# GpSimd takes the bias and residual sums of batch 0 into the scan slots of a decoder layer

## The chip, the cores and the metric

One core of a Trainium2 chip runs one decoder layer in one launch. The metric is the device time of an execution in microseconds. The engines are named as in the profile: PE (TensorE), DVE (VectorE), ACT (ScalarE), POOL (GpSimd), SP (the queue that issues most DMAs).

## The reference, cut to what matters

```python
x = x + attn(layernorm(x))                 # q, k, v, causal softmax, then out @ Wo + bo
x = x + mamba(ctx, z=layernorm(x))         # conv, dt/B/C, selective scan, then y * silu(z)
x = x + ffn(layernorm(x))                  # 16 experts, top 2, and a shared expert
```

x is (4, 512, 512), ctx (4, 512, 256). The scan has 16 states for each of 512 channels. What the change touches is the first line alone: `x + (out @ Wo) + bo` for batch 0, 512 rows of 512 float32 numbers, kept as four tiles of 128 rows.

## The kernel before

Everything is float32 in 128-partition tiles. The stages follow one another: `project` (projections of all batches), `mix` (attention and scan side by side), `close` (output projection of the last batch, gate, norms, shared expert), and then the routed experts.

`mix` is the stage of the change. It runs 128 slots, g = 0 to 127, with three more to drain it. Each engine has its own program with the slots as its loop, and semaphores tie them; nothing reorders the work. A slot holds a piece of attention (one pair of heads, one tile of 128 queries; g % 4 is the tile, and by the causal mask it costs more the higher it is) and two scans of 128 channels by 512 steps.

In slot g, POOL makes product 2g+2 (`weigh`, L763: step size times input times B), adds a state's output into the accumulator (`add`, L771, sum g-3) and makes product 2g+3. The products go into four buffers, so product n waits for scan n-4. DVE takes the maximum of the scores (`top`, L1033), runs scans 2g and 2g+1 (`scan`, L1041; each needs its product from POOL and its decay from ACT) and adds its half of the outputs (`weigh_c`, L1049). ACT makes the decays (L938), the exponentials (L946), copies of transposed tiles (L955), and the weighted copy that POOL's sum reads (L970, two buffers, so copy n waits for sum n-2). PE makes scores (L800, L803), transposes (L818, L857) and the attention sums (L829).

The output projection of batches 0 and 1 rides in the slots, too: L868 from slot 38 on, and ACT copies its half tiles into x1 (L975). Batch 0's are complete at slot 66. Batch 2's is made by PE behind the slots (`project_tail`, L879), batch 3's in `close` (L1514).

The residual has two sums. `with_bias` (L748) is x + bo on POOL, in the place where x lies; `residual` (L1021) adds this to x1 on DVE. For batch 0 `with_bias` runs on POOL in slots 125 to 128 (`EARLY_BIAS`, L740), and `residual` on DVE in slots 128 and 129, with the last two `weigh_c` behind or between them. Then `close` begins on DVE: statistics of batch 0 (L1758, L1764), a square root on ACT (L1671), the normalized rows (L1771), Silu on ACT (L1680), PE's transposes (L1523) and the gate (L1777). On POOL `close` begins with two constants, a wait for the four residuals (L1469), and the bias sums of the other batches, some of them behind waits for ACT and DVE.

SP's queue issues one row of B for all partitions per scan step i (L727), each behind POOL's product 4(i-2)+3. At some steps it issues more: x of batch 0 at step 36, of batch 1 at step 52, the bias bo at step 54 (L717), x of batch 3 at step 56.

Of the kernel before, what the change touches and what calls it, by code (L numbers as in the profile page):

```python
# [631 lines left out]
def mix(nc, d, keep, ctx, first):  # L632
# [3 lines left out]
    def signal(name):  # L636
        return Signal(nc, ctx, "b_" + name)
# [23 lines left out]
    act_da, act_p, act_turn, act_cy = [signal("act_" + n) for n in ("da", "p", "turn", "cy")]  # L661
    dve_max, dve_scan, dve_acc, dve_rinv, dve_out, dve_res = [signal("dve_" + n) for n in ("max", "scan", "acc", "rinv", "out", "res")]
    act_out = signal("act_out")
    pool_dbu, pool_acc, pool_du, pool_xb = [signal("pool_" + n) for n in ("dbu", "acc", "du", "xb")]
    pe_out = signal("pe_out")
    x1 = keep["x1"]
    s_b_all, s_k = keep["s_b_all"], keep["s_k"]
# [21 lines left out]
    def x_rows(b):  # L689
        return (keep["attn"][:, b, :] if b < B - 1 else keep["x1"][b].rearrange("p t c -> p (t c)")).rearrange("p (t c) -> p t c", c=D)  # L690
# [18 lines left out]
    def sync(sp):  # L709
        def load_wo():  # L710
            sp.wait_ge(pool_dbu.sem, pool_dbu.upto(N * KD - 1))
            for k in range(KD):
                sp.dma_start(keep["wo"][:, k, :], d["wo"][k * P:(k + 1) * P, :]).then_inc(keep["s_wo"].sem, keep["s_wo"].tick(k))

        def load_bo():
            sp.wait_ge(pool_dbu.sem, pool_dbu.upto(3 * N * KD - 1))
            sp.dma_start(keep["bo"], d["bo"].rearrange("(a n) -> a n", a=1).broadcast_to([P, D])).then_inc(keep["s_bo"].sem, keep["s_bo"].tick(0))  # L717

        def load_x(b):
            if b < B - 1:  # L720
                sp.wait_ge(pe_out.sem, pe_out.upto(last_out(b, NT - 1)))
            for t in range(NT):
                sp.dma_start(x_rows(b)[:, t, :], d["x"][b, t * P:(t + 1) * P, :]).then_inc(keep["s_x"][b].sem, keep["s_x"][b].tick(1 + t))

        for i in range(2, STEPS):
            sp.wait_ge(pool_dbu.sem, pool_dbu.upto(4 * (i - 2) + 3))
            sp.dma_start(b_all[i % 2][:, :], d["b_flat"][i:i + 1, :].broadcast_to([P, T])).then_inc(s_b_all[i % 2].sem, s_b_all[i % 2].tick(i // 2))  # L727
            if i == N + 1:
                load_wo()
            elif i == 2 * N + 4:  # L730
                load_x(0)
            elif i == 3 * N + 4:
                load_x(1)
            elif i == 3 * N + 6:
                load_bo()
            elif i == 3 * N + 8:
                load_x(B - 1)
        load_x(2)

    EARLY_BIAS = UNITS - 3  # L740

    def bias_at(b, t):
        return NT * (0, 2, 3, 1)[b] + t
# [6 lines left out]
    def gpsimd(pool):  # L750
        def last_batch(j):
            dt, du = [keep[n][B - 1][:, j * T:(j + 1) * T] for n in ("dt", "du")]
            pool.tensor_tensor(du, dt, du, ALU.mult).then_inc(pool_du.sem, pool_du.tick(j))

        def weigh(unit):
            i, k = unit // KD, unit % KD
            if unit == (B - 1) * N * KD:
                pool.wait_ge(pool_du.sem, pool_du.upto(KD - 1))
            if k == 0:
                pool.wait_ge(s_b_all[i % 2].sem, s_b_all[i % 2].upto(i // 2))  # L760
            if unit >= 4:
                pool.wait_ge(dve_scan.sem, dve_scan.upto(unit - 4))
            pool.tensor_tensor(dbu[:, k, :], keep["du"][i // N][:, k * T:(k + 1) * T], b_all[i % 2][:, :], ALU.mult).then_inc(pool_dbu.sem, pool_dbu.tick(unit))  # L763

        def add(n):
            i, t = n // 2, 2 * (n % 2) + 1
            pool.wait_ge(act_cy.sem, act_cy.upto(n))
            if n >= 2:
                pool.wait_ge(pool_acc.sem, pool_acc.upto(n - 2))
            acc = keep["acc"][:, i // N, t * D:(t + 1) * D]  # L770
            pool.tensor_tensor(acc, acc, cy[n % 2][:, :], ALU.add).then_inc(pool_acc.sem, pool_acc.tick(n))  # L771

        pool.wait_ge(first["dve_dt"].sem, first["dve_dt"].upto(4 * B - 1))
        pool.wait_ge(first["pe_rows"].sem, first["pe_rows"].upto(B - 1))
        weigh(0)
        weigh(1)
        for g in range(UNITS + 3):
            if g + 1 < UNITS:
                weigh(2 * g + 2)
            if 0 <= g - 3 < UNITS:  # L780
                add(g - 3)
            if g + 1 < UNITS:
                weigh(2 * g + 3)
            if g < KD:
                last_batch(g)
            if g == EARLY_BIAS:
                pool.wait_ge(keep["s_bo"].sem, keep["s_bo"].upto(0))
            if EARLY_BIAS <= g < EARLY_BIAS + NT:
                with_bias(pool, 0, g - EARLY_BIAS)

    def tensor(pe):
        def scores(unit):
# [221 lines left out]
    def copy_tail(act, t):  # L1014
        act.wait_ge(pe_out.sem, pe_out.upto(HALVES + t))
        act.activation(x1[TAIL][:, t, :], bank[t], ACT.Copy).then_inc(act_out.sem, act_out.tick(HALVES + t))

    def residual(dve, b, t):
        dve.wait_ge(act_out.sem, act_out.upto(last_out(b, t)))
        dve.wait_ge(pool_xb.sem, pool_xb.upto(bias_at(b, t)))  # L1020
        dve.tensor_tensor(x1[b][:, t, :], x1[b][:, t, :], x_rows(b)[:, t, :], ALU.add).then_inc(dve_res.sem, dve_res.tick(NT * b + t))  # L1021

    def normalize(dve, quad):
        b, m = quad // NT, quad % NT
# [4 lines left out]
    def vector(dve):  # L1029
        def top(unit):  # L1030
            n = (unit % NT + 1) * P
            dve.wait_ge(pe_s.sem, pe_s.upto(unit))
            dve.tensor_reduce(neg_max[unit % 2][:, :], sc[:, :, 0:n], AX.X, ALU.max, negate=True).then_inc(dve_max.sem, dve_max.tick(unit))  # L1033

        def scan(unit):
            i, k = unit // KD, unit % KD
            dve.wait_ge(act_da.sem, act_da.upto(unit))
            dve.wait_ge(pool_dbu.sem, pool_dbu.upto(unit))
            if k == 0 and i >= 2:
                dve.wait_ge(pe_y.sem, pe_y.upto(4 * (i - 2) + 3))  # L1040
            dve.tensor_tensor_scan(state[i % 2][:, k, :], da[unit % 2][:, :], dbu[:, k, :], 0.0, ALU.mult, ALU.add).then_inc(dve_scan.sem, dve_scan.tick(unit))  # L1041

        def weigh_c(n):
            i, t = n // 2, 2 * (n % 2)
            dve.wait_ge(pe_y.sem, pe_y.upto(2 * n))
            if n >= 2:
                dve.wait_ge(dve_acc.sem, dve_acc.upto(n - 2))
            acc = keep["acc"][:, i // N, t * D:(t + 1) * D]
            dve.scalar_tensor_tensor(acc, yb[0][:, :], keep["c_flat"][:, i * NT + t:i * NT + t + 1], acc, ALU.mult, ALU.add).then_inc(dve_acc.sem, dve_acc.tick(n))  # L1049

        dve.wait_ge(first["pe_q"].sem, first["pe_q"].upto(4 * B - 1))
        for g in range(UNITS + 3):
            if g % 8 == 0 and g >= 8:
                quad = g // 8 - 1
                dve.wait_ge(act_p.sem, act_p.upto(2 * g - 1))
                dve.reciprocal(rinv[:, :, :], row_sum[quad % 2][:, :, :]).then_inc(dve_rinv.sem, dve_rinv.tick(quad))
            if g < UNITS:
                top(g)
                scan(2 * g)
                scan(2 * g + 1)  # L1060
            if g in (UNITS, UNITS + 1):
                for t in (0, 1):
                    residual(dve, 0, 2 * (g - UNITS) + t)
            if 0 <= g - 2 < UNITS:
                weigh_c(g - 2)
            if spread_in(g) is not None and g < UNITS + 2:
                normalize(dve, spread_in(g))

    return {"sync": sync, "gpsimd": gpsimd, "tensor": tensor, "scalar": scalar, "vector": vector,
            "residual": residual, "res": dve_res, "xb": pool_xb, "with_bias": with_bias, "bias_at": bias_at, "copy_tail": copy_tail, "out_done": act_out, "last_out": last_out, "normalize": normalize, "acc": dve_acc, "pool_acc": pool_acc, "out": dve_out, "y": pe_y, "pv": pe_pv, "p": act_p, "s": pe_s,  # L1070
            "cy": act_cy, "turn": act_turn, "rinv": dve_rinv}


# [256 lines left out]
def close(nc, d, keep, r):  # L1330

    ctx = ExitStack()
    with ctx:
# [130 lines left out]
        def _(pool):  # L1464
# [1 line left out]
            scan["gpsimd"](pool)  # L1466
            pool.memset(eps[:, :], EPS).then_inc(s_const.sem, s_const.tick(0))
            pool.memset(w_r[:, :, :], 0.0).then_inc(s_const.sem, s_const.tick(1))
            pool.wait_ge(dve_res.sem, dve_res.upto(3))  # L1469
            for t in (0, 1):  # L1470
                scan["with_bias"](pool, LAST, t)
            pool.wait_ge(act_silu.sem, act_silu.upto(0))
# [264 lines left out]
        def _(dve):  # L1737
# [12 lines left out]
            def first_stats(b, first, end):  # L1750
                for t in range(first, end):
                    if b == LAST:
                        dve.wait_ge(dve_x1.sem, dve_x1.upto(t))
                    else:
                        if b > 0:
                            scan["residual"](dve, b, t)
                        dve.wait_ge(dve_res.sem, dve_res.upto(4 * b + t))
                    dve.bn_stats(stats[0][b % 2][:, t, :], x1[b][:, t, :]).then_inc(dve_st1.sem, dve_st1.tick(4 * b + t))  # L1758

            def aggregate(b):  # L1760
# [402 lines left out]
```

## Time and profile before

| what | us |
|---|---|
| median of 3 runs (1140.94 to 1142.09) | 1141.82 |
| the profiled execution, own time | 1142.33 |
| its span | 1140.60 |
| PE busy in the span | 1072.7 |
| DVE busy | 827.3 |
| ACT busy | 677.0 |
| POOL busy | 676.1 |

The slots reach from about 143 to 648 us. A duration in the profile is that of one instruction; back to back instructions of one engine overlap a little, so the distance between starts is shorter than the duration. An idle time in brackets stands before the instruction that it precedes, with the instruction that ended it.

### The profile page before, as it was taken

The page shows a single profiled execution, that of the slowest core. Times are in us where ns is not written, and L with a number is a line of the kernel's source. Part 1 is how long each engine was busy: PE and PEld are TensorE (multiplying, and loading weights), DVE is VectorE, ACT ScalarE, POOL GpSimd, SP SyncE. Part 2 cuts the span into 40 slices and gives each one's busy share as a digit, 9 for nine tenths or more (in the row PEclk, how much of TensorE's full clock was granted, in tenths as well). Part 3 has the DMA queues.
Part 4 walks back from the last instruction along what each step waited for, and adds up shares of the span by engine and source line. Part 5 has one row for each costly group of instructions (what it writes and reads, how often), then busy time and mean ns, then how long its engine had stood idle before and what let it go on. Part 6 is the DMA issues. An engine that isn't in the chain of part 4 may idle for free.

```text
span 1140.6 us, 19239 instructions
## 1 busy us (share of the span) xinstructions
PE 1072.7 (94%) x6714; PEld 671.2 (59%) x6714; DVE 827.3 (73%) x1245; ACT 677.0 (59%) x1466; POOL 676.1 (59%) x587
## 2 busy tenths in 40 slices
PE   8999988889999999999998999899999999999993
PEld 3554456666666666666666554444444477777761
DVE  6988699999999999999999966830680144433438
ACT  4876789999999999999999835312011022323220
POOL 2012399999999999999999834102043045555530
PEclk9999989999999999999999999999999999999997
DMA  7210001112111121111221043112225534344329
GB/s 222 93 39 20 21 28 38 38 36 69 38 31 36 29 75 32 35 31 36 84 70 34 11 162 135 74 37 74 76 76 200 182 89 136 129 139 131 71 79 386
DMA packets 51983, 94.77 MB, mean 83 GB/s; under 512 B 9966, under 2 KB 18158, under 8 KB 51888
## 3 DMA queue, kind: packets, MB, share of 16 engines
q1 hardware_dynamic: 44368, 72.82, 19.6%
q0 software_dynamic: 7520, 20.72, 5.9%
q8 instruction: 55, 0.90, 0.3%
q14 instruction: 40, 0.33, 0.1%
HBM read 74.51 MB, written 20.84 MB: 84 GB/s over the span
## 4 chain that ended last, share of the span: by engine, by line
PE 68%; DVE 10%; ACT 8%; POOL 7%; issue 6%; DMA 1%; SPq 0%; DVEq 0%; POOLq 0%; ACTq 0%
PE ps L1558 9%; PE ps L1985 7%; PE ps L1997 7%; PE ps L829 6%; POOL w_all L763 5%; PE ps L857 4%; PE ps L1572 4%; PE ps L818 4%; PE ps L803 4%; PE ps L356 4%; DVE w_all L1041 3%; PE ps L308 3%; PE ps L1581 2%; ACT w_all L955 2%; PE ps L868 2%
## 5 line engine op out<-in xcount | busy, mean ns | idle before, releaser
L763 POOL TENSOR_TENSOR w_all<-w_all 128x512 f32<-128x512 f32 x256 | 322.7, 1288 | 20.2 <-DVE w_all L585 14.8
L1041 DVE TENSOR_TENSOR_SCAN w_all<-ps,w_all 128x512 f32<-128x512 f32 x256 | 298.7, 1205 | 1.2 <-POOL w_all L763 0.6
L938 ACT ACTIVATE ps<-w_all,low 128x512 f32<-128x512 f32 x256 | 177.6, 697 | 1.0 <-DVE w_all L1041 0.8
L857 PE MATMUL ps<-ident,w_all 128*128 128x128 f32 x1024 | 162.0, 281 | 9.6 <-DVE acc L1049 9.4
L946 ACT ACTIVATE w_all<-ps,low 128x128 f32<-128x128 f32 (+3 forms) x256 | 133.1, 531 | 13.6 <-DVE low L1033 13.6
L857 PEld LDWEIGHTS ps<-ident,w_all 128*128 128x128 f32 x1024 | 114.9, 142 | 34.6 <-issue 20.8
L955 ACT ACTIVATE w_all<-ps 128x256 f32<-128x256 f32 (+2 forms) x192 | 102.0, 531 | 22.6 <-PE ps L818 22.3
L2035 DVE COPY attn<-w_all 128x512 f32 x94 | 40.0, 428 | 103.8 <-PE ps L1985 103.0
L1033 DVE TENSOR_REDUCE low<-ps 128x2 f32<-128x256 f32 (+3 forms) x128 | 103.8, 811 | 14.6 <-PE ps L803 14.0
L1558 PE MATMUL ps<-w_all 128*128 128x512 f32 x256 | 112.2, 594 | 0.0
L818 PE MATMUL ps<-ident,w_all 128*128 128x128 f32 x640 | 108.8, 285 | 1.5 <-ACT low L961 1.5
L1491 POOL TENSOR_TENSOR w_all<-w_all 128x512 f32<-128x512 f32 x24 | 29.4, 1225 | 132.5 <-ACT w_all L1693 132.5
L829 PE MATMUL ps<-w_all,low 128*32 128x128 f32 x1280 | 95.0, 278 | 12.1 <-ACT w_all L955 10.8
L803 PE MATMUL ps<-w_all,attn 32*128 32x384 f32 (+3 forms) x512 | 105.1, 487 | 0.0
L1985 PEld LDWEIGHTS ps<-attn 128*128 128x128 f32 x752 | 91.2, 192 | 21.6 <-issue 21.5
L818 PEld LDWEIGHTS ps<-ident,w_all 128*128 128x128 f32 x640 | 70.5, 141 | 51.5 <-issue 48.1
L771 POOL TENSOR_TENSOR acc<-acc,low 128x512 f32<-128x512 f32 x64 | 82.6, 1291 | 24.4 <-ACT low L970 24.3
L1049 DVE SCALAR_TENSOR_TENSOR acc<-ps,low,acc 128x512 f32<-128x512 f32 x128 | 92.7, 725 | 0.0
L1985 PE MATMUL ps<-attn 128*128 128x128 f32 x752 | 91.5, 275 | 0.0
L1948 POOL DMA_INDIRECT sorted_y<-attn,low x47 | 48.5, 1032 | 72.0 <-ACT attn L2025 70.3
L1997 PE MATMUL ps<-w_all,attn 128*128 x188 | 88.4, 593 | 0.4 <-DVE attn L2057 0.4
L829 PEld LDWEIGHTS ps<-w_all,low 128*32 128x32 f32 x1280 | 60.4, 109 | 47.0 <-ACT w_all L955 24.8
(223 smaller groups left out, 1703.9 us busy)
## 6 DMA issues: line engine op xcount, KB each, us to landing
w_all<-b_scratch SPq DMA_DIRECT2D x64, 256.0 KB, 3.3
w_all<-in_w_up SPq DMA_DIRECT2D x16, 512.0 KB, 5.4
w_all<-in_w_down SPq DMA_DIRECT2D x16, 512.0 KB, 6.2
w_all<-sorted_y SPq DMA_DIRECT2D x16, 512.0 KB, 10.5
norms<-attn SPq DMA_DIRECT2D x4, 1024.0 KB, 4.3
out_dram<-acc SPq DMA_DIRECT2D x16, 256.0 KB, 9.0
attn<-in_x SPq DMA_DIRECT2D x3, 1024.0 KB, 6.1
attn<-in_x SPq DMA_DIRECT2D x12, 256.0 KB, 4.6
```

The lines of the kernel that those rows point to most:

```text
L763: pool.tensor_tensor(dbu[:, k, :], keep["du"][i // N][:, k * T:(k + 1) * T], b_all[i % 2][:, :], ALU.mult).then_inc(pool_dbu.sem, pool_dbu ...
L803: last = pe.matmul(sc[:, x, 0:n], keep["attn"][r:r + DH, b, m * T + j * P:m * T + (j + 1) * P], k_4[r:r + DH, b, m // 2, 0:n], start=False ...
L818: last = pe.transpose(tb[:, at:at + P], prob[:, x, off[j] + t * P:off[j] + (t + 1) * P], ident[:, :])
L829: last = pe.matmul(ob[r:r + DH, j * P:(j + 1) * P], keep["v"][:, b * KV + m // 2, t * DH:(t + 1) * DH], prob_t[unit % 2][:, at:at + P], st ...
L857: last = pe.transpose(yb[which][:, k * P:(k + 1) * P], state[i % 2][:, k, t * P:(t + 1) * P], ident[:, :])
L938: act.activation(da[unit % 2][:, :], keep["dt"][i // N][:, k * T:(k + 1) * T], ACT.Exp, scale=keep["a_flat"][:, unit % (N * KD):unit % (N ...
L946: act.activation(prob[:, x, off[j]:off[j] + n], sc[:, x, 0:n], ACT.Exp, bias=neg_max[unit % 2][:, x:x + 1], accum_out=row_sum[unit // 8 % ...
L955: act.activation(prob_t[unit % 2][:, first * n:(first + heads) * n], tb[:, 0:heads * n], ACT.Copy).then_inc(act_turn.sem, act_turn.tick(tu ...
L1041: dve.tensor_tensor_scan(state[i % 2][:, k, :], da[unit % 2][:, :], dbu[:, k, :], 0.0, ALU.mult, ALU.add).then_inc(dve_scan.sem, dve_scan. ...
L1558: last = pe.matmul(bank[m % 2][:, :], s_up[:, k, m * P:(m + 1) * P], norm_t[b][:, k, :], start=(k == 0), stop=(k == 3))
L1985: last = pe.matmul(bank[2 + s][:, f * P:(f + 1) * P], w_up[f][:, k, :], x_t[s][:, k * P:(k + 1) * P], start=(k == 0), stop=(k == KD - 1))
L1997: last = pe.matmul(bank[6 + s1][:, :], h_t[s1][:, f * P:(f + 1) * P], r["w_all"][:, e, KD * FE + f * D:KD * FE + (f + 1) * D], start=(f == ...
```

## The change

POOL does both sums of batch 0. The four `with_bias` move from the end of slots 125 to 128 to the end of slots 106, 107, 110 and 111. The four sums of x1 move from DVE (slots 128 and 129) to POOL, to the end of slots 114, 115, 118 and 119, in a new helper `sum_out` with a semaphore of its own. These are slots with g % 4 of 2 or 3. The bias is loaded at step 50 instead of 54. POOL's wait for the residuals at the start of `close` is gone; the statistics of batch 0 wait for POOL's sums instead.

```diff
-            elif i == 3 * N + 6:
+            elif i == 3 * N + 2:
                 load_bo()
...
-    EARLY_BIAS = UNITS - 3
+    EARLY_BIAS = 3 * 8 * NT + NT + 2 + 4
...
             if g == EARLY_BIAS:
                 pool.wait_ge(keep["s_bo"].sem, keep["s_bo"].upto(0))
-            if EARLY_BIAS <= g < EARLY_BIAS + NT:
-                with_bias(pool, 0, g - EARLY_BIAS)
+            if g % NT >= 2 and 0 <= g - EARLY_BIAS < 2 * NT:
+                with_bias(pool, 0, g // NT % 2 * 2 + g % 2)
+            elif g % NT >= 2 and 2 * NT <= g - EARLY_BIAS < 4 * NT:
+                sum_out(pool, g // NT % 2 * 2 + g % 2)
...
+    def sum_out(pool, t):
+        pool.wait_ge(act_out.sem, act_out.upto(last_out(0, t)))
+        pool.wait_ge(pool_xb.sem, pool_xb.upto(bias_at(0, t)))
+        pool.tensor_tensor(x1[0][:, t, :], x1[0][:, t, :], x_rows(0)[:, t, :], ALU.add).then_inc(pool_res.sem, pool_res.tick(t))
...
-            if g in (UNITS, UNITS + 1):
-                for t in (0, 1):
-                    residual(dve, 0, 2 * (g - UNITS) + t)
...
-            pool.wait_ge(dve_res.sem, dve_res.upto(3))
             for t in (0, 1):
                 scan["with_bias"](pool, LAST, t)
...
                     else:
                         if b > 0:
                             scan["residual"](dve, b, t)
-                        dve.wait_ge(dve_res.sem, dve_res.upto(4 * b + t))
+                            dve.wait_ge(dve_res.sem, dve_res.upto(4 * (b - 1) + t))
+                        else:
+                            dve.wait_ge(scan["pool_res"].sem, scan["pool_res"].upto(t))
```

## Rows read from the trace of the kernel before

**Rows 1.** The page: busy time (share) of each engine, then two of the costliest groups

```profile
PE 1072.7 (94%) x6714; PEld 671.2 (59%) x6714; DVE 827.3 (73%) x1245; ACT 677.0 (59%) x1466; POOL 676.1 (59%) x587
...
L763 POOL TENSOR_TENSOR w_all<-w_all 128x512 f32<-128x512 f32 x256 | 322.7, 1288 | 20.2 <-DVE w_all L585 14.8
L1041 DVE TENSOR_TENSOR_SCAN w_all<-ps,w_all 128x512 f32<-128x512 f32 x256 | 298.7, 1205 | 1.2 <-POOL w_all L763 0.6
```

**Rows 2.** Busy time by stretch: stretch, length, then PE, PEld, DVE, ACT, POOL

```profile
562.42:620.89 58.47, 52.59 (x500) 36.66 (x498) 56.52 (x65) 54.24 (x131) 55.61 (x47) 1.00 0.18 52
...
648.60:664.30 15.70, 15.70 (x119) 9.21 (x118) 10.45 (x16) 6.86 (x13) 8.68 (x9) 1.00 0.01 2
```

**Rows 3.** POOL in order of time: start, us, instruction, idle time before it

```profile
564.88 2.51 POOL L763 TENSOR_TENSOR w_all<-w_all 128x512 f32<-128x512 f32 x2
567.83 1.27 POOL L771 TENSOR_TENSOR acc<-acc,w_all 128x512 f32<-128x512 f32 x1 [0.44 <-ACT w_all L970]
...
588.57 2.50 POOL L763 TENSOR_TENSOR w_all<-w_all 128x512 f32<-128x512 f32 x2
...
595.94 2.52 POOL L763 TENSOR_TENSOR w_all<-w_all 128x512 f32<-128x512 f32 x2
...
603.26 1.28 POOL L771 TENSOR_TENSOR acc<-acc,low 128x512 f32<-128x512 f32 x1 [0.62 <-ACT low L970]
...
619.66 2.50 POOL L763 TENSOR_TENSOR w_all<-w_all 128x512 f32<-128x512 f32 x2
```

**Rows 4.** DVE in order of time: scan pairs of slots 113, 115, 121, idle time

```profile
590.83 2.32 DVE L1041 TENSOR_TENSOR_SCAN w_all<-ps,w_all 128x512 f32<-128x512 f32 x2
...
599.94 2.33 DVE L1041 TENSOR_TENSOR_SCAN w_all<-ps,w_all 128x512 f32<-128x512 f32 x2
...
621.90 2.33 DVE L1041 TENSOR_TENSOR_SCAN w_all<-ps,w_all 128x512 f32<-128x512 f32 x2
...
628.82 0.69 DVE L1027 TENSOR_TENSOR attn<-ps,low 128x512 f32<-128x512 f32 x1
629.88 1.22 DVE L1033 TENSOR_REDUCE low<-ps 128x2 f32<-128x1024 f32 x1 [0.36 <-PE ps L803]
```

**Rows 5.** The chain of waits at the start of slot 124: start, us, what

```profile
633.91 0.41 DVE low L1033
...
636.57 0.65 DVE acc L1049
637.26 0.66 PE ps L857 x4
```

**Rows 6.** The end of the slots: DVE, ACT and PE in order of time

```profile
649.23 3.52 DVE L1021 TENSOR_TENSOR w_all<-w_all,attn 128x512 f32<-128x512 f32 x2
652.68 0.74 DVE L1049 SCALAR_TENSOR_TENSOR acc<-ps,low,acc 128x512 f32<-128x512 f32 x1
653.34 2.35 DVE L1021 TENSOR_TENSOR w_all<-w_all,attn 128x512 f32<-128x512 f32 x2
...
664.32 0.18 DVE L1768 RECIPROCAL low<-low 128x4 f32<-128x4 f32 x1 [5.26 <-ACT low L1671]
...
670.15 0.69 DVE L1021 TENSOR_TENSOR w_all<-w_all,attn 128x512 f32<-128x512 f32 x1 [3.10 <-POOL attn L748]
...
663.50 0.60 ACT L961 ACTIVATE low<-ps 128x512 f32<-128x512 f32 x1 [2.02 <-PE ps L840]
...
653.26 0.49 PE L818 MATMUL ps<-ident,w_all 128*128 128x128 f32 x3
653.59 0.60 PE L857 MATMUL ps<-ident,w_all 128*128 128x128 f32 x4
```

**Rows 7.** SP's queue: the bias load; sizes and median times to landing

```profile
559.17 1.16 SPq L717 DMA_DIRECT2D w_all<-in_bo  x1
...
w_all<-b_scratch SPq DMA_DIRECT2D x64, 256.0 KB, 3.3
...
w_all<-in_bo SPq DMA_DIRECT2D x1, 256.0 KB, 4.1
```

More of the change, by code:

```diff
@@ L663, in mix @@
     act_out = signal("act_out")
-    pool_dbu, pool_acc, pool_du, pool_xb = [signal("pool_" + n) for n in ("dbu", "acc", "du", "xb")]
+    pool_dbu, pool_acc, pool_du, pool_xb, pool_res = [signal("pool_" + n) for n in ("dbu", "acc", "du", "xb", "res")]
     pe_out = signal("pe_out")
@@ L1020, in residual @@
         dve.wait_ge(pool_xb.sem, pool_xb.upto(bias_at(b, t)))
-        dve.tensor_tensor(x1[b][:, t, :], x1[b][:, t, :], x_rows(b)[:, t, :], ALU.add).then_inc(dve_res.sem, dve_res.tick(NT * b + t))
+        dve.tensor_tensor(x1[b][:, t, :], x1[b][:, t, :], x_rows(b)[:, t, :], ALU.add).then_inc(dve_res.sem, dve_res.tick(NT * (b - 1) + t))
     def normalize(dve, quad):
@@ L1069, in mix @@
     return {"sync": sync, "gpsimd": gpsimd, "tensor": tensor, "scalar": scalar, "vector": vector,
-            "residual": residual, "res": dve_res, "xb": pool_xb, "with_bias": with_bias, "bias_at": bias_at, "copy_tail": copy_tail, "out_done": act_out, "last_out": last_out, "normalize": normalize, "acc": dve_acc, "pool_acc": pool_acc, "out": dve_out, "y": pe_y, "pv": pe_pv, "p": act_p, "s": pe_s,
+            "residual": residual, "res": dve_res, "pool_res": pool_res, "xb": pool_xb, "with_bias": with_bias, "bias_at": bias_at, "copy_tail": copy_tail, "out_done": act_out, "last_out": last_out, "normalize": normalize, "acc": dve_acc, "pool_acc": pool_acc, "out": dve_out, "y": pe_y, "pv": pe_pv, "p": act_p, "s": pe_s,
             "cy": act_cy, "turn": act_turn, "rinv": dve_rinv}
```

## The prediction

> **What bounds the kernel now.** I read the page's busy shares and its costliest groups first [rows 1]. The reader is to see that nothing is idle enough to be called cover: three groups, the products and the sums on POOL and the scans on DVE, fill the scan stage, and the whole change lies in that stage and just behind it. The busy time by stretch [rows 2] makes this exact. In slots 106 to 120, 58.47 us long, DVE is busy 56.52 us (97%) and POOL 55.61 us (95%), PE and ACT 90% and 93%. From 648.60 to 664.30 us, behind the last scan, it is the other way round: PE is busy 15.70 of 15.70 us, DVE 10.45, POOL 8.68. So the change takes work from an engine that has room, in a stretch that PE sets, and gives it (twice over, since the bias sums come too) to an engine that has almost none.
>
> The second view is POOL's instructions in order of time [rows 3]. A slot g is three operations: product 2g+2, sum g-3, product 2g+3. Counting back from the last product (255, slot 126), the pair at 564.88 us is products 215 and 216 (end of slot 106, start of 107), the pair at 619.66 us products 243 and 244. From 588.57 to 595.94 six operations follow without a gap, so one takes 1.228 us from start to start: 7.37 / 6. From 564.88 to 619.66 there are 42 operations, 51.6 us of 54.78: POOL's whole idle time is 3.2 us. It lies in front of six sums that wait for ACT's copy; the profile prints 0.44 us for the first and 0.62 for the fifth, 2.86 for all six, less than the distance between starts shows, because the printed duration (1.27 to 1.29 us) overlaps the next start.
>
> The third view is VectorE's instructions in order of time [rows 4]. The reader is to see how early a product is there before its scan. Product 243 starts at 619.66 and ends 1.29 us later, 620.95; its scan is the second of the pair at 621.90, and starts at 621.90 + 2.33 - 1.21 = 623.02. POOL leads by 2.07 us there. For product 227 (588.57 + 1.29 = 589.86) and its scan (590.83 + 1.12 = 591.95) it is 2.09. Product 231 (595.94 + 1.29) and its scan (599.94 + 1.12) have the largest lead, 3.83. The first product of a slot has more lead than the second.
>
> **The change part by part.**
> POOL in the slots. Added: four x + bias sums after slots 106, 107, 110, 111 and four output sums after 114, 115, 118, 119, all 128x512 float32 from two SBUF operands, the form of L763, 1.288 us in the page [rows 1] and 1.228 by starts [rows 3]. All eight lie between product 215 and product 243. Without any idle time, 42 + 8 = 50 operations take 61.4 us, so product 243 starts at 564.88 + 61.4 = 626.3 us and is ready at 627.6 instead of 620.95. Its scan would have begun at 623.02: it is 4.55 us late. The same sum stage by stage: 8 x 1.228 = 9.8 us, less 3.2 us of idle time, less 2.07 us of lead. That the idle time is really used up I checked at each of the six places. At the first, POOL is 1.23 us late and has 0.49 to give back, at the second 1.97 and 0.67, then 3.76 and 0.41, and from there always further behind than ACT's copy. The first scan that comes late is that of product 227: POOL stands 3.35 us behind there with 2.09 us of lead, 1.3 us too late; later 2.7 us at product 235, 3.15 at 241, 4.55 at 243.
>
> The Trainium skill, "Perfetto Trace Analysis", section "GPSIMD Engine Instruction", says that a GpSimd span in a profile isn't to be trusted and that consecutive starts are. The trace agrees here: 42 operations of 1.288 us would be 54.1 us and leave 0.7 us of the 54.78, yet six idle times that sum to 2.86 us are printed in them. By spans the lateness would be 10.3 - 0.7 - 2.07 = 7.5 us; the sum above goes by starts.
>
> What of the 4.55 us lasts. Behind that scan DVE has little to give back: some 0.25 us in two small gaps, the second before the product L1027 at 628.82, then 0.36 us in front of the maximum at 629.88, where it waits for PE's scores [rows 4]. PE's scores for that slot wait for ACT's exponentials, and these for the late maximum, so they come some 3.3 us late and leave DVE to decide. 4.55 - 0.25 - 0.36 = 3.9, taken as 4.0. From there on all engines are shifted alike: the chain of waits goes through DVE at the start of each four slots (L1033, L1041, L1049) and through PE in the rest [rows 5], so nobody has time to catch up. Bounds: at most the full 4.55 from this working, or 9.8 - 3.2 = 6.6 us if the lead were of no use; at least 9.8 - 3.2 - 3.83 = 2.8 if the largest lead were the one that counts, less 0.6 = 2.2, and 0 if the queue took it all.
>
> POOL behind the slots. Removed: four x + bias sums. They cost nothing: products 254 and 255 were ready in time (DVE waited for L763 0.6 us once in 256 times) [rows 1], and POOL's sums 126 and 127 wait for ACT's copies anyway. The wait for the residuals ahead of the last batch's bias sums goes too; POOL reaches it behind sum 127, after the residuals, so nothing. The rest of POOL's order is the same; its next bias sums still wait for ACT's first Silu.
>
> VectorE behind the slots. Removed: four sums, 3.52 + 2.35 = 5.87 us of DVE at 649.23 and 653.34 [rows 6]. What is next behind them is the statistics of batch 0, then DVE sits idle 5.26 us until ACT's L1671. ACT reaches L1671 only behind its copy L961 (663.50), which waits 2.02 us for PE. PE is busy all the time from 648.60 to 664.30 us [rows 2]: the transposes L857 at 653.59 follow L818 at 653.26 as closely as they do one round earlier. So the 5.87 us turn into idle time, 5.26 becoming about 11. If PE did wait for the DVE sum that ends at 653.42, up to 1.7 us would come back (it starts at 652.68; its transposes were through at 650.94). I take 0. Behind it the batch-0 gate waits for POOL's L748 (3.10 us idle on DVE at 670.15), which hangs on Silu and so on PE's shift: unchanged.
>
> SP's queue. The bias load is issued behind the row load of step 50 instead of 54, eight slots earlier than 559.17 us, some 31 us at 3.9 us a slot (58.47 / 15); its only condition (product 191) is met by then. It needs 4.1 us to land [rows 7], so it is there at about 532 us (559 - 31 + 4) and POOL's wait for it at slot 106 (566 us) is free. It is passed by the batch-1 loads of x and three row loads; a row load has two slots, over 7 us, and needs 3.3 [rows 7]. Nothing. Batch 0's x is loaded at step 36. No wait added on POOL there holds: output products of batch 0 end in slot 66.
>
> Sum: +4.0 and -0 us. The profiled execution took 1142.33 us (span 1140.60 and 1.73 around it), so 1146.3; the median of the runs shown is 0.5 us lower, and I give the time against it: 1141.8 + 4.0 = 1145.8 us. The measurement tells about 0.2% (2.3 us) from no change.
>
> **The rivals.**
> A, the forecast, POOL's queue becomes the bound in slots 112 to 121: 1145.8, alone 1144.8 to 1146.6.
> B, the work is hidden: the product's lead or the slack of PE and ACT takes up more than I found, and 0 to 2 us are left, 1141.8 to 1143.8. For it: DVE waited for a product once in 256 scans. Against it: 9.8 us of work into 3.2 of idle and 2.1 of lead.
> C, a faster end: the tail hangs after all on DVE's sums 126 and 127, which stand behind the residuals, and POOL's slots lose less than that gives. Place: PE's transposes at 653.59 and what follows. Price: -1.7 us if sum 126 alone counts, up to -3.9 if the second pair's 2.35 us count as well (less what overlaps), so 1137.9 to 1140.1 with nothing lost in the slots; it decides only where the slots lose less than 1.7 to 3.9. For it: 3.52 us of residuals do delay sum 126. Against it: PE shows no wait there, and it needs B besides.
> D, dearer: a late sum on POOL holds ACT's copy two sums later (two buffers), behind which ACT's decays queue, which the scans need. The tightest place is the sum at 603.26 [rows 3]: 4.64 us late it ends at 609.2, and the copy that needs its buffer comes in that same slot. If it is too late, no lead counts: +6.6, 1148.4.
>
> **How the numbers follow.** A 0.66, B 0.14, C 0.07, D 0.13. Slower by over 0.2%: A and D, 0.79. Within 0.2%: B and the near part of C, 0.17. Faster: the rest of C, 0.04. The range, 1141.6 to 1147.8, takes in A, B's upper part and the near half of D.
>
> **What would show it.** L1041's waits for L763 rise from 0.6 to about 5 us, all in slots 112 to 121; POOL shows no idle time from 566 to 625; product 243 starts at 626 us; the last scan begins near 651.3 instead of 647.3; the stretch from the last scan to the gate stays as long, with DVE's idle time before L1768 near 11 us. I am wrong if the last scan moves by under 2 us (then POOL's operations or leads are mis-sized) or if that stretch shrinks (then C).

## The result, and the profile after

| | before | after |
|---|---|---|
| median, us | 1141.82 (1140.38 to 1142.68, 7 runs) | 1144.69 (1143.37 to 1146.86, 7 runs) |
| the profiled execution, own time | 1142.33 | 1146.86 |
| its span | 1140.60 | 1145.10 |

The ratio after to before is 1.0035 (95% interval 1.0023 to 1.0048): 4.0 us slower, where 4.0 were forecast, and where the medians alone stand 2.9 apart and the two profiled executions 4.5. The interval reaches from 2.6 to 5.5 us and holds all three; the executions of one and the same kernel spread by as much, which is taken up in the last section.

The page of the kernel after: busy times, the shares of the chain that ended last, then the two groups of [rows 1]. In the changed kernel `top` is L1040, `scan` L1048, `weigh_c` L1056, `sum_out` L1023; on PE L857 is L859, L829 is L831, L818 is L820, L803 is L805; the batch-0 reciprocal L1768 is L1773 and the gate L1777 is L1782.

```profile
PE 1072.5 (94%) x6714; PEld 670.8 (59%) x6714; DVE 821.8 (72%) x1241; ACT 676.8 (59%) x1466; POOL 680.8 (59%) x591
...
PE 65%; POOL 10%; DVE 8%; ACT 7%; issue 7%; DMA 2%; SPq 0%; DVEq 0%; POOLq 0%; ACTq 0%
...
L763 POOL TENSOR_TENSOR w_all<-w_all 128x512 f32<-128x512 f32 x256 | 322.0, 1280 | 20.1 <-DVE w_all L585 14.8
L1048 DVE TENSOR_TENSOR_SCAN w_all<-ps,w_all 128x512 f32<-128x512 f32 x256 | 299.1, 1205 | 5.7 <-POOL w_all L763 5.1
```

Four sums fewer on DVE, four more on POOL. The line that matters is the last: the scans' waits for POOL's products went from 0.6 to 5.1 us. Busy time by stretch (columns as in [rows 2], then PE's granted clock), the stretch of slots 106 to 120 first, then four microseconds from PE's wait behind the late scan of product 241 on:

```profile
562.40:621.80 59.40, 51.62 (x491) 35.64 (x490) 55.39 (x64) 53.31 (x125) 59.40 (x49) 1.00 0.17 50
625.00:629.00 4.00, 3.39 (x21) 2.56 (x22) 2.78 (x4) 1.66 (x5) 4.00 (x4) 0.57 0.00 0
```

POOL is busy 59.40 of 59.40 us. In order of time it has no printed idle time until well behind the added operations; the first bias sum, the last output sum and product 243 (with 244):

```profile
567.03 1.27 POOL L748 TENSOR_TENSOR attn<-attn,w_all 128x512 f32<-128x512 f32 x1
...
623.53 1.28 POOL L1023 TENSOR_TENSOR w_all<-w_all,attn 128x512 f32<-128x512 f32 x1
...
627.20 2.51 POOL L763 TENSOR_TENSOR w_all<-w_all 128x512 f32<-128x512 f32 x2
```

DVE in order of time: the maximum of slot 106, the five scans that came late, then two maxima behind them, the second that of the last slot (127).

```profile
563.68 0.96 DVE L1040 TENSOR_REDUCE low<-ps 128x2 f32<-128x768 f32 x1
...
594.21 1.22 DVE L1048 TENSOR_TENSOR_SCAN w_all<-ps,w_all 128x512 f32<-128x512 f32 x1 [1.24 <-POOL w_all L763]
...
606.52 1.22 DVE L1048 TENSOR_TENSOR_SCAN w_all<-ps,w_all 128x512 f32<-128x512 f32 x1 [0.42 <-POOL w_all L763]
...
611.42 1.22 DVE L1048 TENSOR_TENSOR_SCAN w_all<-ps,w_all 128x512 f32<-128x512 f32 x1 [1.23 <-POOL w_all L763]
...
623.69 1.22 DVE L1048 TENSOR_TENSOR_SCAN w_all<-ps,w_all 128x512 f32<-128x512 f32 x1 [0.94 <-POOL w_all L763]
...
628.58 1.22 DVE L1048 TENSOR_TENSOR_SCAN w_all<-ps,w_all 128x512 f32<-128x512 f32 x1 [1.22 <-POOL w_all L763]
...
635.56 1.22 DVE L1040 TENSOR_REDUCE low<-ps 128x2 f32<-128x1024 f32 x1 [0.37 <-PE ps L805]
...
650.73 1.22 DVE L1040 TENSOR_REDUCE low<-ps 128x2 f32<-128x1024 f32 x1 [0.48 <-PE ps L805]
```

The chain of waits from 590 to 634 us says it in one line. Before, the same stretch went round through DVE, PE, ACT and POOL (13% L1041, 12% L829, 11% L763); after, it stays on POOL:

```profile
by line: POOL w_all L763 40.0%; issue 26.0%; POOL acc L771 25.5%; POOL w_all L1023 10.6%; POOLq L769 0.2%
```

The same two maxima, of slots 106 and 127, in the kernel before:

```profile
562.75 0.96 DVE L1033 TENSOR_REDUCE low<-ps 128x2 f32<-128x768 f32 x1
...
645.05 1.23 DVE L1033 TENSOR_REDUCE low<-ps 128x2 f32<-128x1024 f32 x1 [0.47 <-PE ps L803]
```

Where the 4.5 us between the profiled spans come from, in four pieces. The maximum of slot 106 stands at 562.75 before and 563.68 after: 0.93 us from ahead of the change's work. From there to the last slot's maximum it is 82.30 us before (645.05 - 562.75) and 87.05 after: 4.75. From that maximum to the batch-0 reciprocal it is 19.27 both times (664.32 - 645.05, 670.00 - 650.73): nothing. Behind the gate 1.2 us come back. The first piece is no effect of the change: a second profile of the same changed kernel (e8 below) has slot 106's maximum at 562.31, earlier than before's. So in these two executions the slots hold the whole loss.

### The profile page after: what moved, and what is told of

It reads as the page before. It is cut to its first block, busy times and chain, and to the rows that moved or that the text cites. A ratio compares the mean times of both kernels' runs of the same rounds, so it can differ in the third digit from the quotient of the medians.

```text
span 1145.1 us, 19238 instructions
## 1 busy us (share of the span) xinstructions
PE 1072.5 (94%) x6714; PEld 670.8 (59%) x6714; DVE 821.8 (72%) x1241; ACT 676.8 (59%) x1466; POOL 680.8 (59%) x591
## 4 chain that ended last, share of the span: by engine, by line
PE 65%; POOL 10%; DVE 8%; ACT 7%; issue 7%; DMA 2%; SPq 0%; DVEq 0%; POOLq 0%; ACTq 0%
PE ps L1561 9%; PE ps L1990 7%; PE ps L2002 7%; POOL w_all L763 6%; PE ps L831 5%; PE ps L1575 4%; PE ps L356 4%; PE ps L859 4%; PE ps L820 4%; PE ps L805 4%; POOL acc L771 3%; PE ps L308 3%; DVE w_all L1048 3%; PE ps L1584 2%; ACT w_all L957 2%
## 5 line engine op out<-in xcount | busy, mean ns | idle before, releaser
L763 POOL TENSOR_TENSOR w_all<-w_all 128x512 f32<-128x512 f32 x256 | 322.0, 1280 | 20.1 <-DVE w_all L585 14.8
L1048 DVE TENSOR_TENSOR_SCAN w_all<-ps,w_all 128x512 f32<-128x512 f32 x256 | 299.1, 1205 | 5.7 <-POOL w_all L763 5.1
L859 PE MATMUL ps<-ident,w_all 128*128 128x128 f32 x1024 | 162.6, 282 | 12.9 <-DVE acc L1056 12.8
L859 PEld LDWEIGHTS ps<-ident,w_all 128*128 128x128 f32 x1024 | 115.3, 142 | 38.1 <-issue 20.3
L1040 DVE TENSOR_REDUCE low<-ps 128x2 f32<-128x256 f32 (+3 forms) x128 | 103.8, 811 | 14.9 <-PE ps L805 14.1
L820 PE MATMUL ps<-ident,w_all 128*128 128x128 f32 x640 | 109.2, 285 | 1.5 <-ACT low L963 1.5
L831 PE MATMUL ps<-w_all,low 128*32 128x128 f32 x1280 | 95.6, 279 | 11.8 <-ACT w_all L957 10.6
L805 PE MATMUL ps<-w_all,attn 32*128 32x384 f32 (+3 forms) x512 | 105.6, 489 | 0.0
L820 PEld LDWEIGHTS ps<-ident,w_all 128*128 128x128 f32 x640 | 70.8, 142 | 51.7 <-issue 48.5
L1056 DVE SCALAR_TENSOR_TENSOR acc<-ps,low,acc 128x512 f32<-128x512 f32 x128 | 92.7, 724 | 4.2 <-PE ps L859 4.2
L831 PEld LDWEIGHTS ps<-w_all,low 128*32 128x32 f32 x1280 | 60.7, 110 | 46.9 <-ACT w_all L957 24.1
## 6 DMA issues: line engine op xcount, KB each, us to landing
w_all<-sorted_y SPq DMA_DIRECT2D x16, 512.0 KB, 10.8
```

The costliest lines, as they stand in the source:

```text
L805: last = pe.matmul(sc[:, x, 0:n], keep["attn"][r:r + DH, b, m * T + j * P:m * T + (j + 1) * P], k_4[r:r + DH, b, m // 2, 0:n], start=False ...
L820: last = pe.transpose(tb[:, at:at + P], prob[:, x, off[j] + t * P:off[j] + (t + 1) * P], ident[:, :])
L831: last = pe.matmul(ob[r:r + DH, j * P:(j + 1) * P], keep["v"][:, b * KV + m // 2, t * DH:(t + 1) * DH], prob_t[unit % 2][:, at:at + P], st ...
L859: last = pe.transpose(yb[which][:, k * P:(k + 1) * P], state[i % 2][:, k, t * P:(t + 1) * P], ident[:, :])
```

## The experiments

e1, e2, e3, e5 and e8 test the theory that POOL's queue in the slots is the whole cost and the tail is worth nothing, against rivals B and C; the others ask what PE's waits behind the slots are worth. The lengths "of the slots" are always from slot 106's maximum to slot 127's (before: 82.30 us).

**The bias sums alone (e1).** Half of the added operations, all ahead of product 231, the residuals still on DVE.

```diff
-            elif i == 3 * N + 6:
+            elif i == 3 * N + 2:
...
-    EARLY_BIAS = UNITS - 3
+    EARLY_BIAS = 3 * 8 * NT + NT + 2 + 4
...
-            if EARLY_BIAS <= g < EARLY_BIAS + NT:
-                with_bias(pool, 0, g - EARLY_BIAS)
+            if g % NT >= 2 and 0 <= g - EARLY_BIAS < 2 * NT:
+                with_bias(pool, 0, g // NT % 2 * 2 + g % 2)
```

> Half of the change: the four x + bias sums of batch 0 run on POOL in slots 106, 107, 110, 111, the four sums of x1 stay on DVE behind the slots. POOL-queue theory: product 227 is 3.35 us late with 2.09 us of lead, so one scan in slot 113 comes 1.2 to 1.3 us late (the same as in the changed kernel), 0.4 us is given back at the next maximum, and later slots are on time again because POOL's idle time of 1.6 us per eight slots pays the rest: +0.8 us, 1142.6. Rival (each moved operation costs its whole 1.2 us): +4.9 us. Rival (the cost comes from the output sums alone, through ACT's copy buffers): 0 us and no late scan.

Measured: 1142.20 against 1142.79 us, ratio 0.9997 (0.9988 to 1.0006). The 0.8 us that were expected don't show in the time, which came out 0.3 lower; they show in the trace. Its DVE shows one late scan, and by as much as the forecast gave product 227:

```profile
592.97 1.22 DVE L1041 TENSOR_TENSOR_SCAN w_all<-ps,w_all 128x512 f32<-128x512 f32 x1 [1.22 <-POOL w_all L763]
```

The slots take 83.11 us (562.42 to 645.53), 0.81 more, so of 1.22 us 0.4 were given back. Four operations fit into POOL's idle time and lead but for 1.2 us; the other four cost the rest. Behind the slots, the four sums that stayed on DVE take 3.36 us (2.08 + 1.28) where they took 5.87 in the kernel before, while POOL made a bias sum beside them; the reciprocal still stands 19.28 us behind the last maximum, so that gain is worth nothing either.

**The eight operations on 8 of 512 columns (e2).** Everything of the change but POOL's time; the other 504 columns of batch 0's two sums are left out.

```diff
-        pool.tensor_tensor(x_rows(b)[:, t, :], x_rows(b)[:, t, :], keep["bo"], ALU.add)...
+        w = 8 if b == 0 else D
+        pool.tensor_tensor(x_rows(b)[:, t, 0:w], x_rows(b)[:, t, 0:w], keep["bo"][:, 0:w], ALU.add)...
...
-        pool.tensor_tensor(x1[0][:, t, :], x1[0][:, t, :], x_rows(0)[:, t, :], ALU.add)...
+        pool.tensor_tensor(x1[0][:, t, 0:8], x1[0][:, t, 0:8], x_rows(0)[:, t, 0:8], ALU.add)...
```

> The changed kernel with its eight POOL operations in place and all their waits, but each working on 8 of 512 columns (the rest of batch 0's bias and residual sum is left out). POOL-queue theory: eight short operations fit into 3.2 us of idle time, no scan waits for a product; the four DVE sums behind the slots are gone as well and are worth nothing, so 1141.8, 0 +- 0.6 against before. Rival (the tail hangs on DVE's sums 126 and 127): 1.7 to 3.9 us faster than before. Rival (the waits, the order or the earlier bias load cost, not POOL's time): stays at +3 to +4.

Measured: 1141.30 against 1142.79, ratio 0.9991 (0.9979 to 1.0002). The slots take 82.32 us (563.32 to 645.64), as before. Its DVE behind the slots:

```profile
651.58 0.75 DVE L1057 SCALAR_TENSOR_TENSOR acc<-ps,low,acc 128x512 f32<-128x512 f32 x1 [1.66 <-PE ps L860]
...
654.83 0.75 DVE L1057 SCALAR_TENSOR_TENSOR acc<-ps,low,acc 128x512 f32<-128x512 f32 x1 [2.50 <-PE ps L860]
...
664.92 0.18 DVE L1774 RECIPROCAL low<-low 128x4 f32<-128x4 f32 x1 [6.64 <-ACT low L1675]
```

The reciprocal stands 19.28 us behind the last maximum, before 19.27. In place of the sums that left DVE (5.87 us), it has 1.66 + 2.50 + 6.64 = 10.8 us of idle time, before 5.26. By the trace, rival C is out, on this kernel where nothing is late in the slots (the interval alone, 2.4 us faster to 0.2 slower, would leave its near end open), and the tail's edits are worth nothing up to the gate. What is left of the 1.0 us by which the ratio lies under 1 is not settled by its interval.

**The same eight operations spread over 32 slots (e3).** One behind each fourth slot from 99 to 127.

```diff
-    EARLY_BIAS = 3 * 8 * NT + NT + 2 + 4
+    EARLY_BIAS = 3 * 8 * NT + 3
...
-            if g % NT >= 2 and 0 <= g - EARLY_BIAS < 2 * NT:
-                with_bias(pool, 0, g // NT % 2 * 2 + g % 2)
-            elif g % NT >= 2 and 2 * NT <= g - EARLY_BIAS < 4 * NT:
-                sum_out(pool, g // NT % 2 * 2 + g % 2)
+            n = (g - EARLY_BIAS) // NT
+            if g % NT == 3 and 0 <= n < NT:
+                with_bias(pool, 0, n)
+            elif g % NT == 3 and NT <= n < 2 * NT:
+                sum_out(pool, n - NT)
```

> The changed kernel with the same eight operations, but one in every fourth slot (99, 103, 107, 111 bias; 115, 119, 123, 127 sums). POOL-queue theory, stepped with the same idle times and leads: POOL is 2.3 us late at slots 112 and 116, 3.2 at 120 and 124, against 2.0 to 2.1 of lead; scans at most 1.1 to 1.25 us late in slots 121 and 125, none by more; +0.8 to +1.3 us in all, 1142.6 to 1143.1. Rival (it is the amount of work and not its density): as the changed kernel, +3 to +4.

Measured: 1141.65 against 1142.79, ratio 0.9988 (0.9979 to 0.9997). Its late scans:

```profile
625.02 1.22 DVE L1049 TENSOR_TENSOR_SCAN w_all<-ps,w_all 128x512 f32<-128x512 f32 x1 [0.88 <-POOL w_all L763]
...
641.02 1.22 DVE L1049 TENSOR_TENSOR_SCAN w_all<-ps,w_all 128x512 f32<-128x512 f32 x1 [0.63 <-POOL w_all L763]
```

The slots (563.75 to 646.68) take 82.93 us, 0.63 more, where the same eight operations close together cost 4.75: their density counts, not their number. The stage did about as stepped (0.63 for 0.8 to 1.3), the time did not: it was to be about 1 us over before and came out 1.1 under by the medians, 1.4 by the ratio. So something outside the slots is worth 1 to 2 us between kernels. The candidate that the profiles show is where the TensorE clock fell; of that below (e7, e9).

**The eight operations doubled (e5).** Behind each of the eight the same kind of operation once more, into a spare buffer.

```diff
+        def once_more(n):
+            if n >= 3:
+                pool.wait_ge(pool_more.sem, pool_more.upto(n - 3))
+            pool.tensor_tensor(more[n % 3], keep["bo"], keep["bo"], ALU.add).then_inc(pool_more.sem, pool_more.tick(n))
...
                 with_bias(pool, 0, g // NT % 2 * 2 + g % 2)
+                once_more(g // NT % 2 * 2 + g % 2)
...
                 sum_out(pool, g // NT % 2 * 2 + g % 2)
+                once_more(NT + g // NT % 2 * 2 + g % 2)
```

> The changed kernel with a second operation of the same form (into scratch) behind each of the eight: 16 x 1.228 = 19.6 us of added POOL work in slots 106 to 119. POOL-queue theory: idle time (3.2 us) and lead (2.07) are used up once, so the last late scan is 9.8 us later than in the changed kernel, 14.4 us in all; +14.4 to +15.5 against before (more clock losses on PE where it waits), 1157. Rival (each operation's cost is a share of itself, +4 for eight, so +8 for sixteen): 1151.

Measured: 1155.76 against 1141.94, ratio 1.0123 (1.0109 to 1.0138), or 14.0 us, just under the forecast's 14.4 to 15.5 and far from the rival's 8. The slots take 95.97 us (563.49 to 659.46), 13.7 more. Ten scans are late, three of them, the last that of product 243:

```profile
578.83 1.22 DVE L1056 TENSOR_TENSOR_SCAN w_all<-ps,w_all 128x512 f32<-128x512 f32 x1 [1.24 <-POOL w_all L764]
...
595.55 1.22 DVE L1056 TENSOR_TENSOR_SCAN w_all<-ps,w_all 128x512 f32<-128x512 f32 x1 [0.98 <-POOL w_all L764]
...
636.37 1.22 DVE L1056 TENSOR_TENSOR_SCAN w_all<-ps,w_all 128x512 f32<-128x512 f32 x1 [1.23 <-POOL w_all L764]
```

The time came out near the forecast by two errors that cancel. The forecast took 1.228 us for each added operation, but the doubled ones (they read the bias twice) take 1.0 us from start to start, the first from 568.07 to 569.06:

```profile
568.07 1.06 POOL L777 TENSOR_TENSOR w_all<-w_all 128x512 f32<-128x512 f32 x1
569.06 1.29 POOL L764 TENSOR_TENSOR w_all<-w_all 128x512 f32<-128x512 f32 x1
```

So the scan of product 243 is 636.37 - 623.02 = 13.35, less the 0.74 us by which this execution stands later, 12.6 us late and not 14.4. That is 8.0 more than in the changed kernel, all of the second eight: nothing was left to absorb them. The slots lose 1.1 us more than that, and the granted clock fell three times in them (at 595, 619 and 639 us), each time within a microsecond of the end of a PE wait of 2.0 to 2.5 us for `weigh_c`. With e1 and e2 that makes a hinge: 8 operations of next to no length 0.0, 4 operations +0.8, 8 operations +4.75, 16 operations +13.7. Rival B, up to 2 us in all, doesn't fit it.

**The changed kernel again (e8).** No edit; does the loss in the slots repeat?

> The changed kernel once more, on the same chip as the doubled and the spread one. Theory: +4.0 us in the slots alone, up to 0.8 more with a fall of the clock behind PE's waits; ratio 1.003 to 1.005 again.

Measured: 1145.74 against 1141.94, ratio 1.0035 (1.0024 to 1.0047). The slots take 86.98 us (562.31 to 649.29), 4.7 more than before: the loss repeats. On PE, behind the fourth late scan, and the granted clock there:

```profile
624.26 1.11 PE L859 MATMUL ps<-ident,w_all 128*128 128x128 f32 x4 [1.46 <-DVE acc L1056]
```

```profile
624.00:628.00 4.00, 3.74 (x25) 2.90 (x26) 2.78 (x4) 1.55 (x6) 4.00 (x4) 0.57 0.00 0
```

**PE's wait at the gate filled (e7, e9).** In the kernel before, PE waits 2.63 us for the gate's L1777 and then runs at a lower clock. Matmuls whose result nobody reads go between `turn_z(0, 0)` and `turn_z(0, 2)`: six in e7, three in e9.

```diff
             turn_z(0, 0)
+            for n in range(3):
+                pe.matmul(bank[6][:, :], ident[:, :], wo[:, n, :], start=True, stop=True)
             turn_z(0, 2)
```

> The kernel before, with six matmuls of 128x512 into a free PSUM bank (nobody reads them) behind PE's first two transposes of batch 0's z, where PE stands 2.63 us for DVE. Clock theory (TensorE's clock falls to 1.2 GHz behind such a wait, in before's trace with 0.57 granted from 672 to 676 us, and two stages of matmuls then cost 1.5 us more): with PE busy there the granted clock stays at 1.00 at that place, the eight transposes take 1.1 us instead of 1.94; as other traces show the same wait without a fall, the mean gain is under 1.5: -0.3 to -1.5. Rival (the fall has nothing to do with PE's wait): still to be seen at this place in the trace, 0.

Measured: 1141.89 against 1141.94, ratio 1.0006 (0.9998 to 1.0015). Mis-sized: six such matmuls took 5.3 us (twelve records of L1608 from 669.09), twice the wait, and DVE then stood 2.55 us behind PE. In its profile the clock doesn't fall between 160 and 1110 us, at the gate or behind it, but the gate came 2.4 us later, and the time settles nothing: 5 of its 11 executions have a mean granted clock of 0.986 and took 1143.5 us on average, the 6 with 0.990 or more 1141.4. So falls probably still came in some of them; no profile shows where.

> The kernel before with three matmuls of 128x512 (read by nobody) in PE's wait behind its first two transposes of batch 0's z; the fill of six took 5.15 us, twice the wait, so three are to take 2.58 of 2.63. Clock theory: granted clock 1.00 there, the gate no later than before, so where the fall would have come (two of the six traces in which PE has this wait of 2.6 us unfilled: before and spread) 1.5 us are saved, on average -0.3 to -0.8 us. Rival: the fall comes all the same in that stretch and the time is 0 against before.

Measured: 1139.92 against 1142.32, ratio 0.9983 (0.9975 to 0.9992), 1.9 us faster (0.9 to 2.9), where 0.3 to 0.8 were expected. PE of the kernel before around the gate, then its clock; then the same two views of e9:

```profile
672.31 1.94 PE L1523 MATMUL ps<-ident,attn 128*128 128x128 f32 x8 [2.63 <-DVE acc L1777]
674.04 11.23 PE L1514 MATMUL ps<-w_all,attn 128*128 128x512 f32 x24
```

```profile
672.00:676.00 4.00, 3.69 (x11) 2.63 (x12) 3.16 (x6) 0.00 (x0) 0.00 (x0) 0.57 0.72 164
```

```profile
669.65 2.74 PE L1608 MATMUL ps<-w_all,ident 128*128 128x512 f32 x6
672.45 1.16 PE L1523 MATMUL ps<-ident,attn 128*128 128x128 f32 x8
673.44 10.47 PE L1514 MATMUL ps<-w_all,attn 128*128 128x512 f32 x24
```

```profile
672.00:676.00 4.00, 3.95 (x15) 2.06 (x15) 3.78 (x7) 0.00 (x0) 0.00 (x0) 1.00 0.95 249
```

L1523 starts 0.14 us later in e9, but that execution stands 0.13 later already at the batch-0 reciprocal (664.45 and 664.32): the fill just covers the wait. Then the eight transposes take 1.16 instead of 1.94 us and the 24 matmuls 10.47 instead of 11.23: 0.78 + 0.76 = 1.5 us, the price of the fall. No work was removed, 2.74 us of it were added, and the kernel is faster. That it is faster because the fill takes the fall away fits, but is not shown: one profile without the fall could be chance, since four of seven with the wait unfilled have none either (see "Not settled"), and 1.9 us is more than one such fall costs. The fall at 736 us of the kernel before is missing in e9 as well, behind the same wait of 2.05 us that nobody filled. What speaks for it is that none of e9's 12 executions has a mean granted clock of 0.986 or less, and 13 of the 17 of the kernel before beside them have.

**The wait at the gate shortened, alone and with the spread (e4, e6).** The gate waits for POOL's bias sum of batch 1, tile 0, which stands behind POOL's wait for ACT's Silu and two more sums. It goes ahead of that wait, and `bias_at` counts the sums in the new order.

```diff
-        return NT * (0, 2, 3, 1)[b] + t
+        return BIAS_ORDER.index((b, t))
...
+            scan["with_bias"](pool, 1, 0)
             pool.wait_ge(act_silu.sem, act_silu.upto(0))
             for t in (2, 3):
                 scan["with_bias"](pool, LAST, t)
-            scan["with_bias"](pool, 1, 0)
```

> The kernel before, with one change of order on POOL behind the slots: the x + bias sum of batch 1, tile 0, goes ahead of POOL's wait for the first Silu, so DVE's residual of that tile no longer holds the gate of batch 0. Theory (the tail is set by PE, and by this wait on DVE of 3.10 us for which PE stands 2.63 us): PE's idle time before its third and fourth transposes falls from 2.63 to about 0.2, 2.4 us faster, 1139.4, up to 1.5 more where TensorE's clock no longer falls to 1.2 GHz behind that idle time (in before's trace it was granted 0.57 from 672 to 676 us). Rival (given back where DVE gates batch 1): 0.

Measured on the kernel before: 1138.46 against 1142.79, ratio 0.9963 (0.9950 to 0.9977), 4.2 us (2.6 to 5.7) where 2.4 to 3.9 were expected. PE's wait at the gate is 0.44 us instead of 2.63, and the clock stays at 1.00:

```profile
671.24 1.17 PE L1525 MATMUL ps<-ident,attn 128*128 128x128 f32 x8 [0.44 <-DVE acc L1779]
```

> The eight operations spread over every fourth slot, and the bias sum of batch 1, tile 0, ahead of POOL's wait for Silu. Theory (both effects are apart from each other): the slots lose 0.6 us as in the spread kernel's trace, behind them PE's wait of 2.6 us is gone: as the kernel with the bias sum first alone, +0 to +0.6, 1138.5 to 1139. Rival (the DVE sums taken out behind the slots are worth something once PE no longer waits there): under 1138.

Measured with e3's spread: 1137.96 against 1141.94, ratio 0.9971 (0.9962 to 0.9981). The bare time lies just under the rival's bound of 1138, but the kernel before beside it was 0.85 us faster than beside e4, so the ratios count: it is no better than e4 alone (0.9963), and the spread sums bring nothing that can be measured.

**The next wait on PE as well (e10).** In e4 PE still waits 2.06 us ahead of batch 3's transposes; on top of e4's edit `down(0, 1)`, which has its data, goes in front.

```diff
-            turn_z(3, 0)
             down(0, 1)
+            turn_z(3, 0)
```

> The kernel with the bias sum of batch 1, tile 0, first, and on PE the second tile of batch 0's down projection ahead of the transposes of batch 3's z, for which PE stands 2.06 us (ACT's Silu). Theory: the wait is filled with work that has to be done anyway, and the late half of the gate, for which DVE waits 7.60 us, comes 1.8 to 2.1 us earlier: -2.06 us against the kernel with the bias sum first, up to -3.6 where the clock no longer falls behind that wait; 1136.0 to 1136.5, -5 to -6 against before. Rival (batch 3's gate comes 4.9 us later on DVE and moves the router): not faster than 1138.

Measured: 1134.49 against 1142.32, ratio 0.9934 (0.9921 to 0.9947). PE there in e4, and then in e10:

```profile
733.74 1.09 PE L1525 MATMUL ps<-ident,attn 128*128 128x128 f32 x8 [2.06 <-ACT attn L1682]
```

```profile
730.99 7.03 PE L1574 MATMUL ps<-w_all 128*128 128x512 f32 x16
737.86 1.04 PE L1525 MATMUL ps<-ident,attn 128*128 128x128 f32 x8
```

The wait is gone and the clock doesn't fall between 160 and 1110 us (nor does it in e4). This version beats both kernels: 7.5 us (6.1 to 9.0) under before, where 5 to 6 were expected, and, by the two ratios, some 11.5 under after. Against e4 that is 3.3 us by the ratios, within the 2.06 to 3.6 of the forecast; where the 1.3 us beyond PE's wait come from is not shown.

## Why the prediction was right

The mechanism, the place and the time hold: 1145.8 was forecast, 1.0035 x 1141.8 is 1145.8, and the bare median of 1144.7 lies 1.1 under. Step by step:

**POOL's queue.** Held to a tenth of a microsecond. Product 243 was to start at 626.3; it starts at 627.20, and less the 0.93 us by which this execution stands later from slot 106 on, 626.27. Its scan starts at 628.58, before 623.02: 5.56, less 0.93 is 4.63, for 4.55. The first late scan was to be product 227's by 1.3 us: 1.24. The waits for L763 were to rise to about 5 us in slots 112 to 121: 5.1. The bias load, at step 50, landed at 532 us (528.6 + 3.6), as forecast, and POOL shows no wait for it. The Trainium skill, "Perfetto Trace Analysis", section "GPSIMD Engine Instruction", had been the reason to go by starts; the trace agrees, since by the printed durations the scan would have been 7.5 us late.

**What of it lasts.** The step that was mis-sized: 0.6 us given back, 4.0 left. In e1, where one scan was 1.22 us late, 0.4 were given back. In the changed kernel 4.63 us late became 4.75: nothing given back. What stood in its place is on PE:

```profile
625.61 1.12 PE L859 MATMUL ps<-ident,w_all 128*128 128x128 f32 x4 [1.46 <-DVE acc L1056]
626.66 1.50 PE L831 MATMUL ps<-w_all,low 128*32 128x128 f32 x12
628.09 1.07 PE L820 MATMUL ps<-ident,w_all 128*128 128x128 f32 x4
```

The same three in the kernel before:

```profile
621.44 0.66 PE L857 MATMUL ps<-ident,w_all 128*128 128x128 f32 x4 [0.40 <-DVE acc L1049]
622.03 0.85 PE L829 MATMUL ps<-w_all,low 128*32 128x128 f32 x12
622.81 0.66 PE L818 MATMUL ps<-ident,w_all 128*128 128x128 f32 x4
```

The transposes L859 wait 1.46 us for DVE's `weigh_c`, which stood behind the late scan of product 241. From about the end of that wait the granted clock is 0.57 on average over four microseconds, most of them at the lower level of 1.2 GHz, and the matmuls take up to 1.8 times as long. At that wait PE is 625.61 - 621.44 - 0.93 = 3.24 us late; the three groups take 1.5 us more than before, which makes 4.76, and the maxima that follow are 4.75 late. So PE's scores came later than DVE's own 4.63, and there was nothing for DVE to give back. The same row with the same 1.46 us and 0.57 stands in e8. The forecast had PE's scores shifted by the late maximum only; that PE would also wait longer for `weigh_c`, and that the clock would fall behind that wait, it had not. That DVE had less slack than was read would be the other explanation; in e1, where the clock did not fall in the slots, 0.4 us were given back as expected.

**The tail.** Worth nothing, as forecast: 19.27 us both times. DVE behind the slots:

```profile
656.66 0.75 DVE L1056 SCALAR_TENSOR_TENSOR acc<-ps,low,acc 128x512 f32<-128x512 f32 x1 [1.66 <-PE ps L859]
...
659.91 0.75 DVE L1056 SCALAR_TENSOR_TENSOR acc<-ps,low,acc 128x512 f32<-128x512 f32 x1 [2.50 <-PE ps L859]
...
670.00 0.18 DVE L1773 RECIPROCAL low<-low 128x4 f32<-128x4 f32 x1 [6.63 <-ACT low L1674]
```

The idle time was to be 11 us in front of the reciprocal; it is 10.8, but 1.66 and 2.50 of it stand in front of the last two `weigh_c`. PE sets these, and its order was not disturbed by the sums.

**The total.** 0.8 us more in the slots than forecast, and 1.2 less behind the gate. There the kernel before paid a fall of the clock in its profiled execution that the changed one did not:

```profile
677.97 1.16 PE L1526 MATMUL ps<-ident,attn 128*128 128x128 f32 x8 [2.62 <-DVE acc L1782]
678.97 10.47 PE L1517 MATMUL ps<-w_all,attn 128*128 128x512 f32 x24
```

The wait is the same to 0.01 us (2.63 and 2.62), the transposes behind it take 1.94 before and 1.16 after. That the sum 4.0 was hit so well is thus partly luck: two errors of about 1 us cancel, and the second depends on which executions are profiled (in e8's, the stretch behind the reciprocal is 2.8 us shorter than before's, 473.5 for 476.3). Rival D, late copies on ACT that would make it 6.6, would have shown in the slots; they lost 4.75 and 4.7.

**Not settled.** Why the clock falls behind one wait and not behind an equal one, and why it does so more often in one kernel than in another. Of seven profiles with a wait of 2.6 us at the gate, three have the fall there (before, e3, e5) and four not (after, e1, e2, e8). So for e3's 1.1 to 1.4 us under before I have a candidate only: before fell at 736 us too, where it cost 1.5 us more (its 16 matmuls of L1572 took 8.54 instead of 7.03 us), and e3 fell at 728 instead, beside the path. The timed executions point the same way for e1 and e2: 48 of 68 of the kernel before have a mean granted clock of 0.986 or less, only 5 of their 22, though PE's wait at the gate is as long there.

## What to carry to other kernels

Ask of a move to an engine with the lowest total share what that engine has free in the very slots: idle time there plus the lead of its results over their readers is all that is free (here 3.2 + 2.1 us for 9.8), and what goes beyond it lengthens the stage nearly whole (late by 1.2, 4.6 and 12.6 us here, longer by 0.8, 4.75 and 13.7). Work taken off an engine behind the last slot brought nothing, since another engine was busy there without a gap. A short wait on PE in front of matmuls that the end hangs on can be worth more than its length (e4 took 2.2 us of it away and was 4.2 faster): shorten it, or put work with ready data in front of it, before moving sums about.

## What was unexpected of the hardware

Around the end of a PE wait of 1.5 to 2.6 us inside dense work the clock can fall to its lower level for some microseconds (means of 0.57 granted over four), at a cost of about 1.5 us (0.78 + 0.76 at the gate). The timed executions go with the clock, too: of the 68 of the kernel before beside e1 to e10, the 48 with a mean granted clock of 0.986 or less took 1142.6 us on average, the 15 with 0.989 or more 1140.2. So this kernel's own spread, 2.4 us between the two groups, is over half of the effect that was measured, and two profiled executions of one kernel can differ by as much. Executions of like clock can be compared instead, as an estimate, since not all of them ran on one chip: of the 16 of the changed kernel (its own and e8's), the 6 with 0.986 or less took 1146.1 us on average and the 5 with 0.989 or more 1143.9, which is 3.5 and 3.7 us over before. In e9 all 12 runs lie at 0.988 or 0.989 and within 1139.1 to 1141.1. The second surprise is the size of the fill: one matmul of 128 x 512 float32 on 128 columns took 0.9 us (5.3 / 6, and 2.74 / 3 in e9), as two records.
